# Unread products in TensorE's waits around a quantised feed-forward, and four roundings moved from ScalarE to VectorE

## The reference

```
x = act_qdq(x)
up = act_qdq(x @ lpbq_dequant(w_up).T)
gate = act_qdq(x @ lpbq_dequant(w_gate).T)
sig = fixed_qdq_u16(jax.nn.sigmoid(gate))
gate = act_qdq(gate * sig)
o = act_qdq(gate * up)
return o @ lpbq_dequant(w_down).T
```

## Time and profile before

| | us |
|---|---|
| median of the 3 runs shown (2098.89 to 2105.73) | 2099.02 |
| the profiled execution's own time | 2097.34 |
| its span | 2095.6 |
| TensorE products busy | 1925.5 (92%) |
| VectorE busy | 1463.9 (70%) |
| ScalarE busy | 1345.6 (64%) |
| GpSimd busy | 970.4 (46%) |
| mean granted clock | 0.966 |

### The profile page before, as it was taken

How to read it: one execution, slowest core, us unless ns; L and a number is a source line. 1 busy time by engine, 2 the same in 40 slices (tenths; PEclk the granted TensorE clock), 3 DMA queues, 4 the chain that set the end, 5 groups by cost and what they waited for, 6 DMA issues and landing times.

```text
span 2095.6 us, 45982 instructions
## 1 busy us (share of the span) xinstructions
PE 1925.5 (92%) x15235; PEld 1543.7 (74%) x15297; DVE 1463.9 (70%) x3292; ACT 1345.6 (64%) x3094; POOL 970.4 (46%) x1173
## 2 busy tenths in 40 slices
PE   6999999999999999974089999999899999999998
PEld 4877778888888888842078888887677777777776
DVE  5668667777666666657865676767787788677775
ACT  4676567777677677757745666787555555555554
POOL 3555543344344344300026555554366566556565
PEclk8999999999999999997589999999999999999999
DMA  6533300000000000000033434555233333333332
GB/s 182 170 116 110 94 2 2 2 2 2 2 2 2 2 2 2 2 1 1 0 99 99 120 103 109 155 165 160 69 117 122 122 121 124 114 119 122 121 128 91
DMA packets 139168, 161.12 MB, mean 77 GB/s; under 512 B 15340, under 2 KB 99244, under 8 KB 138796
## 3 DMA queue, kind: packets, MB, share of 16 engines
q1 hardware_dynamic: 132780, 153.46, 24.1%
q10 hardware_dynamic: 6160, 4.78, 0.7%
HBM read 119.75 MB, written 38.70 MB: 76 GB/s over the span
## 4 chain that ended last, share of the span: by engine, by line
PE 69%; issue 8%; POOL 8%; DVE 5%; ACT 5%; SPq 2%; DMA 2%; POOLq 0%; ACTq 0%; DVEq 0%
POOL h_lo L2245 7%; PE bank L993 6%; PE score_banks L273 6%; PE bank L1009 6%; PE score_banks L982 5%; PE bank L934 5%; PE bank L935 4%; PE bank L936 4%; PE bank L284 3%; PE score_banks L255 3%; PE score_banks L1902 3%; PE score_banks L1900 3%; PE score_banks L1901 3%; PE bank L1900 2%; PE score_banks L254 2%
## 5 line engine op out<-in xcount | busy, mean ns | idle before, releaser
L2245 POOL TENSOR_TENSOR h_lo<-h,h_hi 128x512 fp32r<-128x512 f32 x264 | 341.1, 1292 | 245.1 <-ACT h_hi L2026 245.0
L1432 POOL TENSOR_TENSOR pw<-ew,rw 128x410 f32<-128x410 f32 x256 | 222.5, 869 | 369.2 <-DVE rw L1282 369.2
L556 DVE TENSOR_REDUCE nmx<-score_banks 128x4 fp32r<-128x512 f32 (+1 forms) x384 | 237.4, 620 | 182.6 <-PE score_banks L255 179.3
L2019 ACT ACTIVATE sl<-score_banks 128x512 f32<-128x512 f32 x264 | 157.8, 598 | 240.1 <-PE score_banks L1902 237.6
L449 ACT ACTIVATE pt<-score_banks 128x512 f32<-128x512 f32 (+1 forms) x384 | 229.4, 599 | 119.8 <-PE score_banks L273 118.9
L2164 DVE TENSOR_TENSOR bank<-score_banks,sl 128x512 f32<-128x512 f32 x264 | 184.1, 697 | 144.2 <-PE score_banks L1902 114.3
L1146 ACT ACTIVATE ew<-score_banks,nmax 128x205 f32<-128x205 f32 x512 | 217.5, 434 | 103.1 <-DVE nmax L1275 101.9
L708 POOL TENSOR_SCALAR_AFFINE_SELECT pt<-pt 128x512 f32<-128x512 f32 x256 | 164.6, 643 | 177.2 <-ACT pt L449 177.2
L273 PE MATMUL score_banks<-q_pack,k_diag 128*128 128x128 f32 (+1 forms) x1536 | 236.8, 278 | 0.1
L273 PEld LDWEIGHTS score_banks<-q_pack,k_diag 128*128 128x128 f32 (+1 forms) x1536 | 188.4, 179 | 45.2 <-issue 36.4
L1900 PE MATMUL score_banks<-x_hi,w_hi 128*128 128x512 f32 x528 | 209.7, 397 | 0.1
(11 more groups left out here) (348 smaller groups left out, 4572.5 us busy)
## 6 DMA issues: line engine op xcount, KB each, us to landing
share_b<-share_rows SPq DMA_DIRECT2D x256, 256.0 KB, 3.1
q_rows<-q_hi SPq DMA_DIRECT2D x96, 128.0 KB, 2.8
q_pack<-q_rows SPq DMA_DIRECT2D x32, 384.0 KB
raw<-in_experts SPq DMA_DIRECT2D x33, 192.0 KB, 3.3
q_rows<-q_lo SPq DMA_DIRECT2D x48, 128.0 KB, 2.7
k_diag<-k_rows SPq DMA_DIRECT2D x64, 96.0 KB
q_pack<-q_rows SPq DMA_DIRECT2D x31, 192.0 KB
k_diag<-k_rows SPq DMA_DIRECT2D x124, 48.0 KB
```

The source lines that it names most:

```text
L556: nc.vector.tensor_reduce(m.nmx[:, b % 2, :, 0, c], m.score[c % 2][:, 0:HC * a.columns].rearrange("p (h k) -> p h k", h=HC)[:, :, 0:a.keys ...
L1432: nc.gpsimd.tensor_tensor(m.pw[:, n, :, :], m.ew[:, n % 2, :, :], m.rw[:, n % 2, :].unsqueeze(2).broadcast_to([128, 2, KW]), ALU.mult)\
L2245: nc.gpsimd.tensor_tensor(m.h_lo[:, k % 3, :], m.h[:, (k + u) % 2, :], m.h_hi[:, k % 3, :].bitcast(F32), ALU.subtract).then_inc(s.los, 1)
```

## The change

Three things are added on TensorE and one is moved.

- `run` of attention 1: `keep_busy(5)` after the second and the fourth scores of each of the first two sequences, and `keep_busy(4)` ahead of the fourth front.
- `ffn_tensor`: `keep_busy(12)` behind the weights' transposes, a wait for the first maximum's reduce on VectorE, and `keep_busy(8)`, all ahead of the first inputs' transposes.
- `ffn_tensor`: a wait for all but the last of the reduces (31 of 32) and `keep_busy(14)`, ahead of the first down products.
- Up blocks 0 to 3 are rounded by VectorE right behind the scales, blocks 4 to 7 by ScalarE where it rounded 0 to 3 before. The loop of the rounding sums on ScalarE has no rounding of up any more.

```diff
     def run():
         front(4, 0, 0)
         for b in range(2):
             for c in range(NC):
                 scores(a, b, b, c)
+                if c % 2 == 1:
+                    keep_busy(5)
             wait(pe, a.s.max_s, b)
             transpose_maxima(a, b, 6)
+        keep_busy(4)
         front(6, 1, 2)
...
+    for n in range(G // 2):
+        nc.vector.tensor_scalar(block(m.up16, n), block(m.up, n), col(FU), None, ALU.mult).then_inc(s.ups, 1)
     for n in range(G):
         round_sigmoid(n)
...
         if n == 1:
             act.wait_ge(s.scaled, 2)
+            act.wait_ge(s.ups, G // 2)
         if n % 2 == 1:
-            round_up(n // 2)
+            round_up(G // 2 + n // 2)
...
     for n in range(G):
         rounding_sum(n, F2)
-        if n < G // 2:
-            round_up(G // 2 + n)
         fill(n)
...
+    keep_busy(12)
+    pe.wait_ge(s.local_max, 1)
+    keep_busy(8)
     transpose_inputs(0)
     pe.wait_ge(s.weights_s, 1)
...
+    pe.wait_ge(s.reduced, 4 * G - 1)
+    keep_busy(14)
     for n in range(G):
         down(n)
         opening(n)
```

More of the change, by code:

```diff
@@ L356, in opening, with keep_busy @@
             value(a, n - 4, 0)
+    def keep_busy(n):
+        for _ in range(n):
+            nc.tensor.matmul(m.mixed[:, 0:128], m.ident[:], m.ident[:], start=True, stop=True)
     def run():
@@ L371, in attention_tensor @@
         return opening, run
-    def keep_busy(n):
-        for _ in range(n):
-            nc.tensor.matmul(m.mixed[:, 0:128], m.ident[:], m.ident[:], start=True, stop=True)
     if a.earlier is None:
```

## The result

The changed kernel takes 2088.81 us (median of 10 runs, 2084.55 to 2094.62), the kernel before on the same chip 2105.78 us (median of 10, 2095.89 to 2115.82). The medians are 17.0 us apart; the ratio of the runs is 0.9928 with a 95% interval of 0.9909 to 0.9947: faster, by 0.72%, some 15 us. The profiled executions are 2086.47 us (span 2084.7) against 2097.34 us (2095.6), 10.9 us apart.

The account below looks back on a forecast made before the run. TensorE was taken to pace most stages, slowed by three low-clock stretches between 913 and 1109 us; 2.8 + 2.7 + 2.4 + 5.6, less 0.3, gave 13.2 us off 2099.02: 2085.8 us, range 2080 to 2094.

Parts of the forecast that it names:

- First part: Feed-forward start: twenty unread products ahead of the projections keep the clock at 2.4 GHz; gain 2.8 us.
- Rival 2: Feed-forward: products nobody reads don't hold or raise the clock; gain only 7.6 us, time 2091.4 us; chance 0.08.
- Second part: Feed-forward's element-wise half: VectorE rounds four up blocks in a wait, relieving ScalarE's loop of rounding sums; gain 2.7 us.
- Rival 3: VectorE's rounding takes 1.76 us a block, delaying the sigmoid loop by 2.6; gain 10.6, time 2088.4 us; chance 0.06.
- Third part: Feed-forward: fourteen unread products ahead of the down products let these run at 2.4 GHz from the first; gain 2.4 us.
- Fourth part: Second attention's opening: twenty-four unread products in short waits prevent the clock's fall at 1091.25; 5.8 less 0.2, gain 5.6 us.
- Rival 1: Second attention's opening: the clock falls low despite the products; gain 7.1 us, time 2091.9 us; chance 0.18.
- Rival 4: Second attention: clock falls in the opening and returns late, slowing later sequences; up to 2115.9 us; chance 0.06.

Follow-up runs that it names:

- e2: kernel before with only the feed-forward's unread products (12 + 8 ahead of the projections, 14 ahead of the down products); 2103.64 us, ratio 1.0.
- e4: changed kernel plus ten unread products between the fourth group of down products and the third front; 2089.29 us, ratio 0.9923 to the kernel before.
- b1: kernel before, unchanged, profiled once more to see where its runs differ; one execution, 2109.40 us.
- e3: kernel before with only the 24 unread products in the second attention's opening; 2109.15 us, ratio 1.0019.
- e1: kernel before with only the move of four up-block roundings from ScalarE to VectorE, no unread products; 2094.03 us, ratio 0.9943.
- p5: changed kernel plus unread products in the first attention's opening, late in the last attention and among the down products; 2088.75 us, ratio 0.9927 to the kernel before.

## Why the prediction held, and where it didn't

The forecast was 2085.8 us against 2099.02 for before, 13.2 us or 0.63% less; measured were 0.72% [0.53, 0.91] less. The sum is right for reasons that are mostly the predicted ones, with one term too large, one missing, and noise of the clock around both. Two things in it are luck. The term that was too large and the one that was missing nearly cancel. And the time, 2085.8 us against 2088.81 measured, starts from a median of three runs, 2099.02, where ten runs have 2105.78; from that one 13.2 us less are 2092.6.

- **First part**, 2.8 us predicted (from the chain's 6.93; the timeline's 6.8 would have given 2.7), 2.6 measured in the changed kernel and in e2. The clock stayed at 2.4 GHz, the first projection came 1.5 us behind the transposes. Rival 2, unread products don't hold the clock, falls.
- **Second part**, 2.7 us predicted, 2.75 in the profile, 3.0 and 2.7 in the stage when tried alone. Rival 3, 1.76 us a block, falls by 0.95.
- **Third part**, 2.4 us predicted. The step was right up to the last product: the first down products at 2.74 us for 24. But the feed-forward gained 6.1 us where 7.9 had been summed for the three parts. The step that failed is the one that asked what is late next: it named VectorE's update and statistics, and not the wait of 2.63 us behind it, in which the clock fell again. e4 filled it and had 7.7 us. Mis-sized by 1.6 us.
- **Fourth part**, 5.8 less 0.2. The stage has 5.6 us less in the mean (237.4 against 231.8), in every one of eight profiles within 0.1 us. Inside it the parts are a little larger each, 0.6 us of excess for the products (by the timelines the third front comes 4.6 us earlier than before, the transposes behind the last products 3.9) and 6.2 gained. The Trainium skill ("TensorE: Matmul & The Clock Gate", "Why this matters for your kernels") asks for no idle time over some 3 us between bursts of products; by that rule the fall would have stayed, since no wait here was near 3 us. The rows contradict it: filling waits of 0.8 to 1.3 us took the fall away. The fall at 1444.3 in b1, with waits of 0.4 us, is a second case against it. Rival 1 falls.
- **Not in the sum**: 2.6 us in the experts (587.0 in the mean of the six profiles with the old stream, 584.4 of seven with the short one), from the length of ScalarE's stream: 2.0 for the stall, and in the mean 0.6 for the clock that was low behind it in two of the six. The prediction said "all later stages follow from there by semaphores, so I let a lead won here last to the end". Neither half is true: a stage far behind gained of its own, and the last attention varies by more than the lead.
- **Rival 4**, a clock that falls and comes back late, wasn't seen in the opening. Its mechanism is real, though, 350 us further on: e3's profile was at 1.2 GHz for 61 us with TensorE never idle for most of it, and lost 20 us.

The stages that repeat give 6.1 + 5.6 + 2.6 = 14.3 us, against some 15 measured and 10.9 between the two profiles first compared. Of the experiments' medians that sum explains the changed kernel, but not its parts: e1's ratio is 12 us where its stages say 5.5, e2's 3.3 us would be a ratio of 0.9984, just outside its interval (lower end 0.9985), and e3 is 4 us slower where its stage says 5.6 faster. In the profiles the difference lies in the start and the last attention, and there mostly in how long the clock was low. Is that chance, or does the moment at which the last attention is reached decide? Profiles with a lead from the opening have 186.7 to 205.8 us there, those without 186.0 to 194.5; the ranges overlap and fourteen profiles don't settle it. It stays open.

## What to carry to other kernels

Where TensorE's clock falls in short waits, products that nobody reads, sized to the wait, hold it: at five places (both openings, ahead of the projections, ahead of and among the down products) they kept or brought back the clock, at a price of some 0.6 us in the second opening and none that shows in the feed-forward (in the first opening it can't be told), in every profile but p5's, where it was low at two moments around the projections all the same. Count in the trace where the added instructions ran: the late products missed the wait that they were meant for and ran a second time in the first attention, for 2.3 us. Look at the next wait behind the one that is filled, because the clock falls there next, and judge each filling by the length of its own stage in several profiles; medians of the whole kernel hid a gain of 5.6 us behind a scatter of 20. And where instructions are moved between engines, look at the ends of loops far behind: three instructions more or fewer moved a stall from one engine to another, and that was 2 us of the kernel's time.

## What was new about the hardware

- Three waits satisfied at once, in ScalarE's stream 800 us ahead of a loop's end, put a stall on ScalarE there (VectorE then waited 3.91 us for it) that was on VectorE otherwise (2.66 us, "issue"). The experts took 3.2 us more, some 2.0 for the stall and the rest behind a low clock from 1795.0 to 1798.4.
- The granted clock fell at 1444.3 us with TensorE's waits at 0.4 us or less, and stayed low for 61 us in another run while TensorE was busy for 60.0 of 61 us (1457 to 1518).
- Time at the low clock goes with 0.30 to 0.34 us of time per us over the whole kernel (lines through the runs of five kernels) and 0.35 in the last attention (fourteen profiles). In the element-wise half it can cost next to nothing, since TensorE works 0.89 us of 72 there.
